# Loading and measuring the image ahead of a frequency-domain layer, and eight even halves on the way back

## The chip, the cores and the metric

One core of a Trainium2 chip runs the whole program in one launch. The metric is the device time of one execution in microseconds: median 3509.49 us of three runs (3507.69 to 3510.06). All times inside an execution are counted from the start of the profiled span.

## The reference

The input x has the shape (4, 128, 128, 16). Four residual blocks follow, each behind a group normalisation (8 groups of two channels, mean and variance over image and pair):

```python
x = x + _L0_conv_ref(_gn(x), h0, numerators, denumerator)   # 2D rational filter, applied by FFT
x = x + _L1_conv_ref(_gn(x), Wq, bq, ...)                    # 8x8 patches, products in frequency
x = x + _L2_conv_ref(_gn(x), filters, bias)                  # 3x3 convolution
x = x + _L3_conv_ref(_gn(x), h0, numerators, denumerator)    # as the first, other weights

def _L0_conv_ref(x, h0, numerators, denumerator):
    a = jnp.pad(denumerator, ..., constant_values=1.0); b = jnp.pad(numerators, ...)
    h = irfft2(rfft2(b, s=(128, 128)) / rfft2(a, s=(128, 128)))
    H_full = h0 + rfft2(h, s=(256, 256))[0]
    Y = einsum('...hwi,ijhw->...hwj', rfft2(x, s=(256, 256)), H_full)
    return irfft2(Y)[..., :128, :128, :]
```

## The kernel before

The program is a row of stages. Each stage has a block of its own with one instruction list per engine (PE, ACT, DVE, POOL, and SP, which issues DMAs); between stages all engines meet at a barrier, and the semaphores of the stage are cleared. Inside a stage the order on an engine is the order of the list, and a wait on a semaphore holds everything behind it on that engine. DMAs issued by SP travel in queue q1, those issued by ACT in q10; both use the same 16 DMA engines.

**build_filters** (0 to 637 us) computes the filters of both layers in 16 units: per unit ACT splits spectra out of PSUM (den, sq), POOL and DVE form the quotient, PE turns it back to lags and to slots, ACT puts the slots into `stage` (L400), and SP stores `stage` to DRAM, eight pieces of 512 KB a unit (L239). The two units of pair p are `stage[:, 0]` and `stage[:, 1]`; the last unit is pair 7, half 1. At its end SP waits for all stores to land (L255).

**filtered_layer** runs as layer 0 and as layer 1. Its start: SP loads the image (layer 0 only; in layer 1 the local convolution leaves it in SBUF) and the constants (L682 to L686); ACT loads the filters of the first two groups, eight DMAs of 256 KB (L938); DVE takes the statistics, 32 bn_stats (L870); PE averages them over partitions (L755, L759) with small DVE operations between, ACT takes the root (L941), DVE the reciprocal (L886). Then 32 rows: PE transposes a channel (L745), DVE normalises it into `cols` (L892), PE transforms it (L766), ACT copies the row out (L946), and SP stores it as two DMAs of 136 KB (L660; some late rows share the work with ACT). Four row buffers are in the ring: row v waits until the DMAs of row v - 4 have landed. From these rows in DRAM the shifted copies are loaded, and 32 groups of convolution products follow on PE (L774, L788), each with filters fetched by SP (L562).

On the way back the last products are moved across partitions by eight small DMAs (L670). PE (L821) forms 16 units, each an even half and an odd half of four products, into PSUM banks; six even halves are done ahead of the moved products, and then six odd halves and ten whole units; DVE adds each unit to the image (L930).

**to_patches** and **patch_mixer** (the second block) lie between the layers, and **local_conv** before layer 1: 16 tiles, each a convolution on PE (L1818, L1822), a sum on DVE (L1858), a transposition (L1809), and a copy to the image on ACT (L1790).

Of the kernel before, what the change touches and what calls it, by code (L numbers as in the profile page):

```python
# [123 lines left out]
GROUPS = L // 4  # L124
# [18 lines left out]
def build_filters(nc, io, scratch, const):  # L143
# [10 lines left out]
    with ExitStack() as ctx:  # L154
# [7 lines left out]
        den = sb("den", [128, DEEP, 8, 2, PAIRS])  # L162
        sq = sb("sq", [128, DEEP, 8, 2, PAIRS])
        mag = sb("mag", [128, DEEP, 8, PAIRS])
        rec = sb("rec", [128, DEEP, 8, PAIRS])
        straight = sb("straight", [128, DEEP, 8, 2, PAIRS])
        crossed = sb("crossed", [128, DEEP, 8, 2, PAIRS])
        nyq = sb("nyq", [128, 2, PAIRS])
        spec = sb("spec", [L, 2, 2, PAIRS, FW])
        lags = sb("lags", [128, 2, 2, L // LAGS, C, LAGS], R32)  # L170
        stage = sb("stage", [128, 2, GROUPS, 4, KB, 4])
# [16 lines left out]
        stored = [sem(f"stored{k}") for k in range(2)]  # L188
# [30 lines left out]
        def _(sp):  # L219
# [13 lines left out]

            def store(pair, jp, piece):

                if piece == 0:
                    sp.wait_ge(far_out, KB * (2 * pair + jp + 1))
                at = slice(GROUPS // PIECES * piece, GROUPS // PIECES * (piece + 1))
                sp.dma_start(scratch["filters"][at, :, pair, jp].rearrange("g p n -> p g n"),  # L239
                             stage[:, jp, at].rearrange("p g m k s -> p g (m k s)")).then_inc(stored[jp], 16)  # L240
# [199 lines left out]
        def _(dve):  # L440
# [67 lines left out]
            for g in range(8):  # L508
                lags_rest(UNITS - 1, g)

# [49 lines left out]

def load_filters(eng, filt, scratch, layer, g, k, q):
# [23 lines left out]
def filtered_layer(nc, layer, image, source, spare, filt, scratch, const, out_dram, tag):  # L585
# [22 lines left out]
    with ExitStack() as ctx:  # L608
        sb, ps, sem = allocators(nc, ctx, tag)
        ident = sb("ident", [128, 128])  # L610
        average = sb("average", [128, 128])
        fwd_w = sb("fwd_w", [L, 2, 128])
        inv_w = sb("inv_w", [128, 2, L])
        eps = sb("eps", [128, 1])
        stats = sb("stats", [128, 32, 6])
# [15 lines left out]
        direct = [ps(f"direct{k}", [128, B, FAR + 2]) for k in range(2)]  # L631
# [3 lines left out]
        img = [a[:].rearrange("p (j g) t -> p j (g t)", j=4) for a in (*acc[0], *acc[1])]  # L635

        image_in = [sem(f"image_in{b}") for b in range(B)]
        consts_in, stats_ready, zeroed = sem("consts_in"), sem("stats_ready"), sem("zeroed")
# [101 lines left out]
        def _(pe):  # L740
# [7 lines left out]
            pe.wait_ge(consts_in, 48)  # L748
            if source is not None:
                for b in range(B):  # L750
                    pe.wait_ge(image_in[b], 16)
            for i in range(4):
                turn_channel(i)
            pe.wait_ge(stats_ready, 1)
# [107 lines left out]
        def _(dve):  # L862
# [3 lines left out]
            for n in range(32):  # L866
                b, g = n // 8, n % 8
                if source is not None and g == 0:
                    dve.wait_ge(image_in[b], 16)
# [63 lines left out]
        def _(act):  # L933
            if source is not None:
                act.wait_ge(image_in[B - 1], 16)
# [985 lines left out]
```

## Time and profile before

| | us |
|---|---|
| median of three runs | 3509.49 |
| the profiled execution | 3497.7 |
| its span | 3495.9 |
| PE busy in the span | 3244.6 (93%) |
| filter stage, up to the first instruction of layer 0 | 0 to 637 |
| layer 0: start and rows / groups / way back | 637 to 706 / to 1122 / to 1160 |
| local convolution, up to the first instruction of layer 1 | to 2980.5 |
| layer 1: start and rows / groups / way back | to 3045 / to 3453 / to 3491 |

A window row gives busy time and instruction count per engine, then the granted TensorE clock (1.00 is 2.4 GHz, 0.50 is 1.2 GHz), the mean busy share of the 16 DMA engines, and GB/s. A timeline row gives the start, the duration from the first start to the last end of merged instructions, engine, line, operation, count, and in brackets the idle time before and what ended it. SPq and ACTq are DMA issues of SP and ACT.

### The profile page before, as it was taken

To read this page: it belongs to the slowest core of one execution; us is meant where nothing else is said; L and a number is where in the kernel's file an instruction comes from. 1 tells how busy PE (TensorE), PEld (TensorE's weight loads), DVE (VectorE), ACT (ScalarE), POOL (GpSimd) and SP (SyncE) were. 2 spreads that over 40 slices of the span, in tenths; PEclk is the share of its full clock that TensorE was granted. 3 is DMA by queue.
4 is the path that set the end of the run, shared out by engine and by line. 5 is a ranking of instruction groups with operands and counts; after the bars stand their busy time and mean duration, and the time that the engine had idled before them with its cause. 6 is when DMAs were issued, how large, how long until landed. Compare 5 with 4: busy or idle time off the path is not lost. (4 is left out here: it accounts for less than half of the span.)

```text
span 3495.9 us, 82613 instructions
## 1 busy us (share of the span) xinstructions
PE 3244.6 (93%) x37272; PEld 2672.4 (76%) x37272; DVE 1568.7 (45%) x1926; ACT 1680.7 (48%) x1763; POOL 1257.6 (36%) x1018
## 2 busy tenths in 40 slices
PE   7999999589998699999899999999989997799998
PEld 6999998379998566666688776666668773489998
DVE  6787877411111434444765444344665444411112
ACT  3666665356553344444554434444454440355551
POOL 6888886055552102222440001222271000165550
PEclk9999999899999899999999999999999998899999
DMA  0333334787777321222133331222222344777776
GB/s 18 114 116 118 122 122 140 215 209 197 198 196 183 106 94 66 79 73 75 70 109 97 109 121 62 83 73 73 73 73 73 91 126 87 176 204 202 203 202 163
DMA packets 259721, 428.86 MB, mean 123 GB/s; under 512 B 28263, under 2 KB 106601, under 8 KB 257897
## 3 DMA queue, kind: packets, MB, share of 16 engines
q1 hardware_dynamic: 244346, 396.86, 38.9%
q10 hardware_dynamic: 15024, 26.72, 2.4%
q8 instruction: 293, 4.80, 0.6%
q14 instruction: 58, 0.48, 0.0%
HBM read 306.07 MB, written 113.77 MB: 120 GB/s over the span
## 5 line engine op out<-in xcount | busy, mean ns | idle before, releaser
L138 PE MATMUL m_bank<-xn,w 128*128 128x512 f32 x1536 | 619.2, 403 | 31.8 <-DVE m_store L1597 11.7
L139 PE MATMUL m_bank<-xn,w 128*128 128x512 f32 x1536 | 603.1, 393 | 0.0
L140 PE MATMUL m_bank<-xn,w 128*128 128x512 f32 x1536 | 602.8, 392 | 0.0
L774 PE MATMUL c_acc<-c_shifted,filt 128*32 128x256 f32 (+8 forms) x11264 | 457.2, 317 | 9.5 <-issue 9.4
L774 PEld LDWEIGHTS c_acc<-c_shifted,filt 128*32 128x32 f32 x11264 | 442.7, 159 | 20.3 <-issue 16.9
L568 POOL TENSOR_TENSOR filt<-filt 64x1408 f32<-64x1408 f32 x64 | 259.6, 4056 | 473.1 <-DMA filt<-filters_dram 473.1
L581 ACT ACTIVATE filt<-filt 64x2048 f32<-64x2048 f32 (+3 forms) x256 | 422.6, 1754 | 14.3 <-DMA filt<-filters_dram 10.6
L138 PEld LDWEIGHTS m_bank<-xn,w 128*128 128x128 f32 x1536 | 291.3, 190 | 172.9 <-issue 76.0
L129 ACT ACTIVATE w<-raw_weights 128x2048 fp32r<-128x2048 f32 x96 | 373.0, 3886 | 103.3 <-PE m_bank L140 102.0
L133 DVE TENSOR_TENSOR w<-raw_weights,w 128x2048 fp32r<-128x2048 f32 x86 | 334.0, 3883 | 159.0 <-ACT w L129 159.0
L140 PEld LDWEIGHTS m_bank<-xn,w 128*128 128x128 f32 x1536 | 291.1, 190 | 62.9
L139 PEld LDWEIGHTS m_bank<-xn,w 128*128 128x128 f32 x1536 | 291.6, 190 | 59.9 <-issue 2.2
L1689 POOL TENSOR_TENSOR m_sums<-m_sums,m_store 128x512 f32<-128x512 f32 x48 | 139.0, 2896 | 519.6 <-DVE m_store L1554 519.6
L908 DVE TENSOR_TENSOR c_both<-c_acc,c_odd 128x256 f32<-128x256 f32 x64 | 36.0, 563 | 469.5 <-ACT c_odd L969 469.5
L482 DVE RECIPROCAL f_rec<-f_mag 128x256 f32<-128x256 f32 x144 | 226.9, 1586 | 22.5 <-POOL f_mag L518 20.7
L129 ACT ACTIVATE m_w_out<-m_qf 128x1024 fp32r<-128x1024 f32 x64 | 131.6, 2056 | 203.3 <-PE m_bank L140 195.9
L1686 POOL TENSOR_TENSOR m_sums<-m_store 128x512 f32<-128x512 f32 x8 | 24.2, 3023 | 526.7 <-DVE m_store L1554 526.7
L297 PE MATMUL f_ring<-f_inv_h,f_spec 128*64 128x128 f32 x1024 | 199.2, 277 | 14.0 <-POOL f_spec L541 14.0
L1547 DVE TENSOR_TENSOR m_pf<-m_bank,m_qf 128x512 f32<-128x512 f32 x128 | 82.5, 686 | 289.1 <-PE m_bank L1267 289.1
L138 PE MATMUL m_bank<-m_u_out,m_w_out 128*128 128x512 f32 x512 | 204.3, 399 | 7.2 <-DVE m_u_out L133 7.2
L133 DVE TENSOR_TENSOR m_w_out<-m_qf,m_w_out 128x1024 fp32r<-128x1024 f32 x64 | 129.0, 2016 | 181.6 <-ACT m_u_out L129 181.6
L969 ACT ACTIVATE c_odd<-c_acc 128x256 f32<-128x256 f32 x64 | 33.1, 517 | 353.6 <-PE c_acc L774 353.6
(182 smaller groups left out, 6763.7 us busy)
## 6 DMA issues: line engine op xcount, KB each, us to landing
c_shifted<-spectrum_dram SPq DMA_DIRECT2D x256, 270.0 KB, 3.9
filters_dram<-f_stage SPq DMA_DIRECT2D x128, 512.0 KB, 3.6
filt<-filters_dram SPq DMA_DIRECT2D x240, 256.0 KB, 4.7
raw_weights<-in_L_conv_Wq SPq DMA_DIRECT2D x16, 2048.0 KB, 8.7
raw_weights<-in_L_conv_Wk SPq DMA_DIRECT2D x16, 2048.0 KB, 8.6
raw_weights<-in_L_conv_Wv SPq DMA_DIRECT2D x16, 2048.0 KB, 8.6
m_qf<-in_L_conv_Wout SPq DMA_DIRECT2D x128, 256.0 KB, 3.9
spectrum_dram<-c_shifted SPq DMA_DIRECT2D x116, 136.0 KB, 2.4
```

Of the source, the lines that this page charges most:

```text
L129: return eng.activation(out, src, ACT.Copy)
L133: return eng.tensor_tensor(out, src, high.bitcast(F32), ALU.subtract)
L138: pe.matmul(out, w[0], x[0], start=first, stop=False)
L139: pe.matmul(out, w[0], x[1], start=False, stop=False)
L140: return pe.matmul(out, w[1], x[0], start=False, stop=last)
L297: nc.tensor.matmul(lo, re, inv_h[:, 0], start=True, stop=False)
L482: nc.vector.reciprocal(rec[:, s, 0:f], mag[:, s, 0:f]).then_inc(rec_ready, 1)
L568: return eng.tensor_tensor(both, even, odd, ALU.add)
L581: return eng.activation(filters_of(filt, k, phases, 1, column, first), filters_of(filt, k, phases, 0, 1 - column, first), ACT.Copy, scale= ...
L774: mm = nc.tensor.matmul(acc[k % 2][phase][32 * s:32 * s + 32, 0:B, LAGS * kb:HALF], filt[:, k, phase, :, :, 4 * kb + s].rearrange("p j c - ...
L1547: op = nc.vector.tensor_tensor(pf[:, k, d], freq[K][d][:], qf[:, k, d], ALU.mult)
L1689: nc.gpsimd.tensor_tensor(sums[:, head], sums[:, head], store[:, head, d], ALU.add).then_inc(added_up, 1)
```

## The change

- Layer 0's image is loaded by SP at the end of the filter stage, once POOL has finished the last quotient; DVE takes the statistics behind its last work there. The constants `ident`, `average`, `fwd_w` come in at the stage's beginning.
- The scratch tensors den, sq, straight, crossed, mag, rec become views of the image, and spec a view of the later `raw_weights`.
- The filter stage no longer waits for its last stores: the last unit's eight pieces are issued by the next stage, four by SP and four by ACT. The first two groups' filters in layer 0 are fetched by ACT behind rows 5 to 12, with a wait for all stores ahead of the first.
- In layer 1 the statistics are taken by DVE within the local convolution, the constants are loaded there, and the first filters are fetched by SP at the layer's start.
- PE averages the statistics first and transposes channels 0 to 3 between the steps; ACT does one root ahead.
- On the way back eight even halves are done ahead (`direct` grows to a whole bank each).

```diff
+def store_filters(eng, scratch, stage, stored, pair, jp, piece):
+    n = GROUPS // 8
+    return eng.dma_start(scratch["filters"][n * piece:n * piece + n, :, pair, jp].rearrange("g p n -> p g n"),
+                         stage[:, jp, n * piece:n * piece + n].rearrange("p g m k s -> p g (m k s)")).then_inc(stored[jp], 16)
...
-        den = sb("den", [128, DEEP, 8, 2, PAIRS])
...
+        held = image[:].rearrange("p b w c -> p (b w c)")
+        den, sq, straight, crossed = (held[:, 2 * size * n:2 * size * (n + 1)].rearrange("p (s f t n) -> p s f t n", s=DEEP, f=8, t=2)
+                                      for n in range(4))
...
             for pair in range(1, UNITS // 2):
                 step(pair, 0)
                 step(pair, 1)
-            for jp in range(2):
-                for piece in range(PIECES):
-                    store(UNITS // 2 - 1, jp, piece)
-            for jp in range(2):
-                sp.wait_ge(stored[jp], 16 * PIECES * UNITS // 2)
+            for piece in range(PIECES):
+                store(UNITS // 2 - 1, 0, piece)
+            sp.wait_ge(spec_ready, UNITS)
+            for b in range(B):
+                sp.dma_start(image[:, b], io["x"][b]).then_inc(image_in[b], 16)
+            sp.wait_ge(tables_in, 48)
...
             for g in range(8):
                 lags_rest(UNITS - 1, g)
+            for b in range(B):
+                dve.wait_ge(image_in[b], 16)
+                image_stats(nc, image, stats, b).then_inc(stats_ready, 1)
+            dve.wait_ge(stats_ready, B)
...
+def image_stats(nc, image, stats, b):
+    for g in range(8):
+        op = nc.vector.bn_stats(stats[:, 8 * b + g], image[:, b, :, 2 * g:2 * g + 2])
+    return op
...
+    LAST_PAIR, FETCH_AT = 7, 5
-    AHEAD = 6
+    AHEAD = 8
...
-        direct = [ps(f"direct{k}", [128, B, FAR + 2]) for k in range(2)]
+        direct = [ps(f"direct{k}", [128, B, L]) for k in range(2)]
...
         @block.sync
         def _(sp):
-            if source is not None:
-                for b in range(B):
-                    sp.dma_start(image[:, b], source[b]).then_inc(image_in[b], 16)
-            sp.dma_start(ident[:], const["ident"]).then_inc(consts_in, 16)
-            sp.dma_start(average[:], const["average"]).then_inc(consts_in, 16)
-            sp.dma_start(fwd_w[:], const["fwd_w"]).then_inc(consts_in, 16)
+            if staged is not None:
+                stage, stored = staged
+                for at in range(4):
+                    store_filters(sp, scratch, stage, stored, LAST_PAIR, 1, at)
+            else:
+                for k in range(EARLY):
+                    for q in range(4):
+                        load_filters(sp, filt, scratch, layer, k, k, q).then_inc(filt_in[k], 16)
             sp.dma_start(inv_w[:], const["inv_w"]).then_inc(inv_in, 16)
...
-            for i in range(4):
-                turn_channel(i)
-            pe.wait_ge(stats_ready, 1)
             nc.tensor.matmul(tot.rearrange("p (n s) -> p n s", s=2), average[:],
                              stats[:].rearrange("p n (s k) -> p n s k", k=3)[:, :, :, 1], start=True, stop=True).then_inc(sum_ready, 1)
+            turn_channel(0)
+            turn_channel(1)
             pe.wait_ge(mean_ready, 1)
             pe.wait_ge(spread_ready, 1)
             nc.tensor.matmul(tot, average[:], spread[:].rearrange("p n s -> p (n s)"), start=True, stop=True).then_inc(sum_ready, 1)
+            turn_channel(2)
+            turn_channel(3)
...
         @block.scalar
         def _(act):
-            if source is not None:
-                act.wait_ge(image_in[B - 1], 16)
-            for k in range(EARLY):
-                for q in range(4):
-                    load_filters(act, filt, scratch, layer, k, k, q).then_inc(filt_in[k], 16)
+            if staged is not None:
+                stage, stored = staged
+                for at in range(4, 8):
+                    store_filters(act, scratch, stage, stored, LAST_PAIR, 1, at)
+            act.wait_ge(zeroed, 1)
+            nc.scalar.activation(warm[:], eps[:], ACT.Sqrt)
             act.wait_ge(var_ready, 1)
...
                 nc.scalar.activation(rows[:, v % 4, :, :, LAGS:], freq[v % 2].rearrange("p b (t q) -> p b q t", q=2), ACT.Copy).then_inc(rows_ready, 1)
+                if staged is not None and FETCH_AT <= v < FETCH_AT + 4 * EARLY:
+                    if v == FETCH_AT:
+                        for jp in range(2):
+                            act.wait_ge(stored[jp], 16 * 8 * (LAST_PAIR + 1))
+                    k, q = divmod(v - FETCH_AT, 4)
+                    load_filters(act, filt, scratch, layer, k, k, q).then_inc(filt_in[k], 16)
...
+            def take_stats(b):
+                dve.wait_ge(moved, 4 * b + 4)
+                image_stats(nc, image, stats_2, b).then_inc(image_ready, 1)
+
             for t in range(16):
...
+                if t % 4 == 2 and t > 4:
+                    take_stats(t // 4 - 1)
+            take_stats(B - 1)
+            dve.wait_ge(image_ready, B)
```

In `build`, stage, the tables and the semaphores `stored` are now opened around `build_filters` and handed to the layer; `img[u % 6]` becomes `img[u % 8]`, with the two banks of `direct` as the seventh and eighth.

## Rows read from the trace of the kernel before

**Rows 1.** Windows: length, busy us of PE, PEld, DVE, ACT, POOL, clock, DMA share, GB/s.

```profile
80.00:600.00 520.00, 502.32 (x6530) 469.95 (x6531) 416.41 (x632) 340.64 (x663) 426.63 (x681) 1.00 0.36 121
...
640.00:680.00 40.00, 26.11 (x100) 16.79 (x100) 32.20 (x100) 10.40 (x17) 6.34 (x2) 0.74 0.87 235
```

**Rows 2.** Timeline, ACT, 610 to 669: start us, us, engine, line, operation, idle before.

```profile
610.98 11.19 ACT L400 ACTIVATE f_stage<-f_ring 128x512 f32<-128x512 f32 x16 [1.79 <-PE f_ring L314]
...
649.34 5.31 ACTq L562 DMA_DIRECT2D filt<-filters_dram  x8
...
654.74 1.28 ACT L941 ACT_TABLE_LOAD   x1 [32.56 <-issue]
...
656.03 0.32 ACT L941 ACTIVATE c_std<-c_var,c_eps 128x32 f32<-128x32 f32 x1
...
668.30 0.60 ACT L946 ACTIVATE c_shifted<-c_acc 128x512 f32<-128x512 f32 x1 [0.71 <-PE c_acc L766]
```

**Rows 3.** Timeline of SP's queue (SPq), 622 to 694, the stores by narrow windows.

```profile
622.20 2.02 SPq L239 DMA_DIRECT2D filters_dram<-f_stage  x3
...
625.60 2.73 SPq L239 DMA_DIRECT2D filters_dram<-f_stage  x2
...
629.73 1.36 SPq L239 DMA_DIRECT2D filters_dram<-f_stage  x1
...
660.93 32.42 SPq L660 DMA_DIRECT2D spectrum_dram<-c_shifted  x46
```

**Rows 4.** Timeline of DVE, same stretch.

```profile
609.23 0.69 DVE L133 TENSOR_TENSOR f_lags<-f_ring,f_lags 128x512 fp32r<-128x512 f32 x1 [1.05 <-ACT f_lags L129]
...
641.83 10.55 DVE L870 BATCH_NORM_STATS2 c_stats<-image 128x6 f32<-128x256 f32 x32 [4.53 <-DMA image<-in_x]
...
656.78 6.47 DVE L892 TENSOR_SCALAR raw_weights<-c_acc,c_mean,c_rstd 128x128 f32<-128x128 f32 x20
```

**Rows 5.** Windows of 2 us, 602 to 671, for the DMA columns.

```profile
602.00:604.00 2.00, 2.00 (x40) 2.00 (x38) 0.70 (x2) 0.81 (x2) 0.00 (x0) 1.00 0.37 124
...
624.00:626.00 2.00, 0.00 (x0) 0.00 (x0) 0.00 (x0) 0.00 (x0) 0.00 (x0) 1.00 1.03 339
...
641.00:643.00 2.00, 0.00 (x0) 0.00 (x0) 1.17 (x4) 0.00 (x0) 0.00 (x0) 0.50 1.00 418
...
655.00:657.00 2.00, 0.41 (x2) 0.30 (x2) 0.95 (x4) 1.34 (x2) 0.00 (x0) 1.00 1.07 199
...
669.00:671.00 2.00, 2.00 (x9) 1.18 (x8) 2.00 (x7) 0.69 (x2) 0.00 (x0) 1.00 0.96 216
```

**Rows 6.** Timeline of DVE, ACT, SP: local convolution's end, start of layer 1.

```profile
2942.40 1.11 DVE L1858 SCALAR_TENSOR_TENSOR l_res<-l_acc,l_bias,l_xt 128x512 f32<-128x512 f32 x1 [2.77 <-PE l_acc L1822]
...
2979.14 0.60 ACT L1790 ACTIVATE image<-l_turn 128x512 f32<-128x512 f32 x1 [0.81 <-PE l_turn L1809]
...
2980.55 0.34 SPq L683 DMA_DIRECT2D c_ident<-const_ident  x1
...
2981.12 10.20 DVE L870 BATCH_NORM_STATS2 c_stats<-image 128x6 f32<-128x256 f32 x31
...
2995.87 6.47 DVE L892 TENSOR_SCALAR spare<-c_acc,c_mean,c_rstd 128x128 f32<-128x128 f32 x20
```

**Rows 7.** Timeline of PE and DVE on the way back, and two clock windows.

```profile
1133.46 25.87 PE L821 MATMUL c_acc<-c_inv_w,filt 128*128 128x128 f32 x208 [4.11 <-DMA filt<-raw_weights]
...
3463.66 26.39 PE L821 MATMUL c_acc<-c_inv_w,filt 128*128 128x128 f32 x208 [4.83 <-DMA filt<-spare]
...
3475.80 0.69 DVE L930 TENSOR_TENSOR image<-image,c_acc 128x512 f32<-128x512 f32 x1 [1.10 <-PE c_acc L821]
...
1131.00:1132.00 1.00, 0.00 (x0) 0.00 (x0) 0.00 (x0) 0.00 (x0) 0.00 (x0) 0.84 0.08 6
...
3462.00:3463.00 1.00, 0.00 (x0) 0.00 (x0) 0.00 (x0) 0.00 (x0) 0.00 (x0) 0.99 0.00 0
```

**Rows 8.** Timeline of POOL in the filter stage.

```profile
589.17 0.72 POOL L526 TENSOR_TENSOR f_crossed<-f_crossed 128x256 f32<-128x256 f32 x1
```

More of the change, by code:

```diff
@@ L161, in build_filters @@
         respread = sb("respread", [L, 2, 2 * 128], R32)
-        den = sb("den", [128, DEEP, 8, 2, PAIRS])
[L163 to L167, printed above, removed]
+        ident_0, average, fwd_w, stats = tables
+        held = image[:].rearrange("p b w c -> p (b w c)")
+        size = DEEP * 8 * PAIRS
+        den, sq, straight, crossed = (held[:, 2 * size * n:2 * size * (n + 1)].rearrange("p (s f t n) -> p s f t n", s=DEEP, f=8, t=2)
+                                      for n in range(4))
+        mag, rec = (held[:, size * n:size * (n + 1)].rearrange("p (s f n) -> p s f n", s=DEEP, f=8) for n in range(8, 10))
         nyq = sb("nyq", [128, 2, PAIRS])
-        spec = sb("spec", [L, 2, 2, PAIRS, FW])
+        spec = spare[:].rearrange("p a r n -> p (a r n)").rearrange("p (k c n f) -> p k c n f", k=2, c=2, n=PAIRS)
         lags = sb("lags", [128, 2, 2, L // LAGS, C, LAGS], R32)
-        stage = sb("stage", [128, 2, GROUPS, 4, KB, 4])
         early = stage[:].rearrange("p j g m k s -> p (j g m k s)")
@@ L187, in build_filters @@
         far_ready, far_out = sem("far_ready"), sem("far_out")
-        stored = [sem(f"stored{k}") for k in range(2)]
+        tables_in, stats_ready = sem("tables_in"), sem("stats_ready")
+        image_in = [sem(f"image_in{b}") for b in range(B)]
         block = ctx.enter_context(nc.Block())
@@ L582, in lower_columns, with filtered_layer @@
                           scale=1.0 if column else -1.0)
-def filtered_layer(nc, layer, image, source, spare, filt, scratch, const, out_dram, tag):
+def filtered_layer(nc, layer, image, tables, staged, spare, filt, scratch, const, out_dram, tag):
     N_BATCHES = GROUPS // RING
@@ L865, in _ @@
             nc.vector.memset(odd[:, :, :, 0:1], 0.0).then_inc(edge_set, 1)
[L866 to L869, printed above, removed]
-                op = nc.vector.bn_stats(stats[:, n], image[:, b, :, 2 * g:2 * g + 2])
-            op.then_inc(stats_ready, 1)
             sample = stats[:].rearrange("p n (s k) -> p n s k", k=3)
@@ L1716, in _, with local_conv @@
                     normalise(half, n)
-def local_conv(nc, io, image, scratch, const, tag):
+def local_conv(nc, io, image, tables, scratch, const, tag):
     with ExitStack() as ctx:
@@ L1871, in build @@
     }
-    build_filters(nc, io, scratch, const)
     with nc.sbuf_tensor("mean1", [128, B], F32) as mean, nc.sbuf_tensor("rstd1", [128, B], F32) as rstd:
         with nc.sbuf_tensor("raw_weights", [128, 2, 8, 512], F32) as raw:
-            with nc.sbuf_tensor("image0", [128, B, L, C], F32) as image:
+            with ExitStack() as ctx:
+                sb, ps, sem = allocators(nc, ctx, "a_")
+                image = sb("image0", [128, B, L, C])
+                tables = tables_tensors(sb)
+                stored = [sem(f"stored{k}") for k in range(2)]
+                with nc.sbuf_tensor("stage", [128, 2, GROUPS, 4, L // 8, 4], F32) as stage:
+                    build_filters(nc, io, image, raw, tables, stage, stored, scratch, const)
                 with filter_tensor(nc, "filt0") as filt:
-                    filtered_layer(nc, 0, image, io["x"], raw, filt, scratch, const, None, "c0_")
+                    filtered_layer(nc, 0, image, tables, (stage, stored), raw, filt, scratch, const, None, "c0_")
             with nc.sbuf_tensor("xn", [128, 2, 8, N], R32) as x:
@@ L1881, in build @@
                     patch_mixer(nc, io, x, (w0, w1), mean, rstd, raw, scratch, const, "m_")
-    with nc.sbuf_tensor("image1", [128, B, L, C], F32) as image:
-        local_conv(nc, io, image, scratch, const, "l_")
+    with ExitStack() as ctx:
+        sb, ps, sem = allocators(nc, ctx, "e_")
+        image = sb("image1", [128, B, L, C])
+        tables = tables_tensors(sb)
+        local_conv(nc, io, image, tables, scratch, const, "l_")
         with filter_tensor(nc, "filt1") as filt:
             with nc.sbuf_tensor("spare", [128, 2, 8, 512], F32) as spare:
-                filtered_layer(nc, 1, image, None, spare, filt, scratch, const, out, "c3_")
+                filtered_layer(nc, 1, image, tables, None, spare, filt, scratch, const, out, "c3_")
 INPUTS = {
```

37 lines of the change are left out of this document (18 added, 19 removed).

## The prediction

> **What bounds the kernel now.** I read the busy time by stage first, then the chain of waits, then each engine's timeline around the places that the diff touches. The groups of convolution products and the second block are PE work that the change leaves alone. The stretches with slack are the seams. In the filter stage PE is busy for 502 of 520 us; in the 40 us at layer 0's start only 26 of 40, at a mean clock of 0.74 [rows 1].
>
> Read as a chain, that seam is one thing after the other: ACT puts the last slots out until 622.17 (610.98 + 11.19) [rows 2]; SP then issues eight stores of 512 KB, the last ending at 631.09 [rows 3], and waits until they land; only then is the image loaded; DVE, waiting for it, takes statistics from 641.83 to 652.38 and begins to normalise at 656.78 [rows 4]. From there to the first products the row phase is paced by row stores: SP issues 46 without a pause, 0.70 us each [rows 3]. So the bound at this seam is DMA, then DVE, then DMA.
>
> At layer 1 the same statistics stand alone between the local convolution's last copy (ends at 2979.74) and the normalisation at 2995.87 [rows 6]. On the way back PE waits 4.11 and 4.83 us for the moved products, and then runs 208 matmuls in 25.87 and 26.39 us [rows 7].
>
> **Part 1, layer 0's start: -25.9 us.** The image is loaded behind the eight stores of the last unit but one. Their transfer ends in the window 602 to 604 (124 GB/s there against 339 at full rate, so at 602.7); the image, 4.19 MB at 418 GB/s, takes 10.0 us [rows 5], to 612.7. DVE is free at 609.92 and needs 32 x 0.33 = 10.55 us [rows 4], so it ends at 620.5, under ACT's slots, which end at 622.17. The cover is thin, 1.7 us on DVE and about 5 on the image's last quarter (wanted at 617.8); past that, each microsecond late costs one.
>
> The next stage then starts at 622.17 plus a barrier. From ACT's end at 2979.74 to the first DMA of layer 1 is 0.81 us [rows 6], so 622.98. The stores of the last unit are no longer waited for, but four of them now stand in ACT's list ahead of the root. This is the term without a row. From below: on one queue the fifth store begins to issue 3.4 us after the first (622.20 to 625.60). From above: all eight take 8.9 us (to 631.09) [rows 3]; two queues that drain together at one queue's rate could hold ACT that long. I take 5.6, nearer to the lower end, since four and not eight stand in the ring. Behind them come the table load 1.28, the extra root 0.32, and from the true root to the first normalisation 0.75 (656.03 to 656.78) [rows 2, 4]: 622.98 + 5.6 + 2.35 = 630.93 against 656.78, a gain of 25.85 (22.5 to 28.0). PE and DVE's own chain isn't later: from the end of the statistics to 656.78 were 4.40 us, so about 627.4, or 629.2 with two more channels transposed in between. The new root ahead of the true one saves nothing here, since ACT is late anyway.
>
> **Part 2, the first filters move into the row phase: +8.3 us.** Before, eight fetches of 256 KB were issued at 649.34 [rows 2] while PE and DVE were in the statistics. Now they come behind rows 5 to 12. The wait ahead of them is free: row 5 comes 11.5 us behind the first normalisation (668.30 against 656.78 [rows 2, 4]), so about 642, and 4.19 MB of stores at 339 GB/s [rows 5] are done near 636. ACT's issue costs 5.31 / 8 = 0.66 us in an idle of 0.71 per row [rows 2]: nothing, but for some tenths. The filters themselves are wanted only by row 19.
>
> What isn't free is the transfer. Alone, the fetch ran at 199 GB/s with the DMA engines' share at 1.07; the row stores ran at 216 GB/s and 0.96 [rows 5]. From above it costs its whole length, 2.10 MB / 199 GB/s = 10.5 us. From below nothing: a share of 0.96 for one queue need not mean that two queues can't overlap. I take the additive case with the little room there is, 0.11 of each microsecond over some 20 us: 10.5 - 2.2 = 8.3. The row stores queue behind it on SP, ACT's row copies wait for stores four rows back, and PE for ACT; nothing later in the phase is idle enough to win it back.
>
> The Trainium skill bears on this (DMA: Bandwidth & Descriptors, section "Issuing engines are not separate DMA queues"): DMAs of different issuers end on the same 16 engines and interleave, and a second issuer saves issue time alone. The two shares of rows 5 fit it, but no row shows these two transfers at once. By the rule part 2 costs its 8 to 10 us; without it, nothing.
>
> **Part 3, layer 1's start: -8.2 us.** Three of the four images' statistics run in DVE's idle time under the convolution: 8 x 0.33 = 2.64 us against 2.77 us idle per tile [rows 4, 6]. If they run over, PE wants the next sum only one tile of 3.88 us (1.11 + 2.77) later, so still nothing. The last image's eight wait for ACT's last copy: 2979.74 + 2.7 = 2982.45, plus the barrier 0.81, plus the chain of 4.40 us as in layer 0 [rows 4]: 2987.66 against 2995.87. The four constants' loads and ACT's fetch no longer stand in front; the fetch, now on SP's queue, is issued in 8 x 0.66 us, before the first row is ready. Bounds 7.0 (PE still cold from its pause) to 9.5 (PE no longer behind four channels).
>
> **Part 4, the way back, twice: -7.8 us.** Two more even halves, 16 matmuls, move into the wait. Warm, a whole unit of 16 takes 0.69 + 1.10 = 1.79 us [rows 7]; that much goes per layer. The wait itself ends with the moved products, as before. PE's idle time shrinks to 2.32 and 3.04 us. The clock counts here: 208 matmuls at the warm pace are 23.2 us, so 2.6 and 3.2 of the 25.87 and 26.39 are paid at the 1.2 GHz level. It fell 2.35 us behind PE's last matmul in layer 0 (1133.46 - 4.11 = 1129.35; 0.84 granted from 1131 to 1132, so at 1131.7) and 4.15 us in layer 1 (0.99 in the last microsecond to 3463) [rows 7]. In layer 0 I let it stay up (1.79 + 2.6 = 4.4), in layer 1 count the half (1.79 + 1.6 = 3.4). Bounds: 3.6 if it falls in both, 9.4 if in none. DVE's adds of 0.69 still fit under halves of 0.89. The wider `direct` banks cost nothing that a row shows.
>
> **The sum.** 25.85 - 8.3 + 8.2 + 7.8 = 33.6 us off the profiled execution's 3497.7 (span 3495.9): 3464.1. The runs' median, 3509.49, stands 11.8 above the profiled one; taking the same off it gives **3475.9 us**, which I forecast.
>
> **Rivals.**
> - *The fetch hides.* Two queues overlap and part 2 costs nothing: gain 41.9, **3467.6**. For it: the share is summed over queues, and 1.07 shows that their packets can overlap. Against: at 1.07 the rate was lower, 199 GB/s.
> - *ACT is held to the end.* Its four stores are out only after 8.9 us, the fetch costs all of 10.5, the clock falls in both waits: 22.5 - 10.5 + 7.0 + 3.6 = 22.6, **3486.9**. For it: issues of 1.36 us each at the end of the burst [rows 3].
> - *The statistics don't fit.* The image lands late, the stage is held and part 1 shrinks. With half of it gone the gain is 20.7, **3488.8**; with all, 7.7, **3501.8**. Against: 5 us of room.
> - *Slower: the moved scratch tensors slow the filter stage.* den to rec now lie in the image, spec in the later weights' buffer. POOL is busy for 426.6 of 520 us there [rows 1]; if its operations were dearer at the new places, 512 us of stage would stretch. The gain of 33.6 is gone from 6.6% on; at 10%, 51 us are lost: **3527**. Against it: POOL's operations take the same 0.72 us [rows 8] on tensors at quite different places.
>
> **Chances.** Forecast (3471 to 3482) 0.47; fetch hidden (3462 to 3471) 0.28; ACT held (3482 to 3488) 0.14; statistics late (3488 to 3502) 0.05; slower 0.04; about nothing in all, 0.02. No change means within 0.2%, 7.0 us, about what a measurement of this kernel can tell. So faster 0.94, same 0.02, slower 0.04. The range of 8 in 10 is 3463 to 3487: the first three cases but for their outer edges.
>
> **What would show it.** Part 1: DVE's bn_stats end before ACT's last slot copy, and the first normalisation comes 8 us (5.7 to 11.5) behind the stage's start. Part 2: row stores at a pitch well over 0.70 us, or a longer landing, in the rows behind row 5; if the pitch holds, the first rival is right. Part 3: the first normalisation of layer 1 about 8 us behind ACT's last image copy. Part 4: 192 matmuls behind the wait, in 21.5 us if the clock reads 1.00 throughout. The forecast is wrong if the filter stage's end moves off 622, or if the distance from the first normalisation to the first product of layer 0 shrinks or grows by more than part 2 says.

## The result, and the profile after

The kernel after took 3461.34 us (median of four runs, 3458.84 to 3469.81) against 3508.59 (four runs, 3500.11 to 3510.06): a ratio of 0.9868, with an interval of 0.9841 to 0.9895. Two later timings gave 0.9868 (0.9831 to 0.9905) and 0.9889 (0.9847 to 0.9930). All 14 runs of the kernel after in these three have a median of 3468.1, all 25 of the kernel before (in these and beside the kernels of the experiments) one of 3508.5: some 40 us faster, where I forecast 33.6. The first timing, which I had forecast at 3475.9, lies just under my range of 3463 to 3487.

Single profiles scatter by 10 us and more, so the steps are read from distances inside a profile. First the seam at layer 0, in windows of the kernel after (columns as in [rows 1]):

```profile
80.00:600.00 520.00, 502.32 (x6530) 469.93 (x6531) 416.37 (x632) 340.80 (x663) 426.24 (x681) 1.00 0.36 121
612.00:652.00 40.00, 32.56 (x177) 23.27 (x176) 29.25 (x94) 18.31 (x32) 2.73 (x1) 0.96 0.74 233
```

The filter stage is as it was, POOL's 426 us too, so the rival in which the moved scratch tensors slow it is dead. The seam has PE busy for 32.6 of 40 us at a clock of 0.96, where [rows 1] had 26.1 at 0.74. The timeline of ACT, SP's queue and DVE there, against [rows 2 to 4]:

```profile
610.91 11.06 ACT L410 ACTIVATE stage<-f_ring 128x512 f32<-128x512 f32 x16 [1.78 <-PE f_ring L324]
622.86 3.64 ACTq L146 DMA_DIRECT2D filters_dram<-stage  x4
626.53 1.28 ACT L954 ACT_TABLE_LOAD   x1 [4.55 <-issue]
...
627.93 0.30 ACT L956 ACTIVATE c_std<-c_var,c_eps 128x32 f32<-128x32 f32 x1
...
598.64 4.31 SPq L264 DMA_DIRECT2D a_image<-in_x  x4
...
632.81 35.70 SPq L682 DMA_DIRECT2D spectrum_dram<-c_shifted  x46
...
609.77 10.54 DVE L577 BATCH_NORM_STATS2 a_stats<-a_image 128x6 f32<-128x256 f32 x32
...
624.98 0.23 DVE L899 TENSOR_REDUCE c_var<-c_direct 128x32 f32<-128x64 f32 x1 [0.59 <-PE c_direct L778]
...
628.66 9.01 DVE L907 TENSOR_SCALAR raw_weights<-c_acc,c_mean,c_rstd 128x128 f32<-128x128 f32 x28
```

The statistics end at 620.3, under ACT's copies of the last slots. The variance is there at 625.2, but ACT comes to the root only at 627.93, behind its four stores. The normalisation starts at 628.66 (656.78 before). SP's 46 row stores take 35.70 us where [rows 3] had 32.42. PE's first product of the layer, before and then after, ends the row phase:

```profile
706.12 8.10 PE L774 MATMUL c_acc<-c_shifted,filt 128*32 128x256 f32 x176
```

```profile
680.27 7.29 PE L795 MATMUL c_acc<-c_shifted,filt 128*32 128x256 f32 x174
```

It comes 49.34 us behind the first normalisation before (656.78 to 706.12) and 51.61 after (628.66 to 680.27). Layer 1's start, against [rows 6]:

```profile
2957.05 0.60 ACT L1815 ACTIVATE e_image<-l_turn 128x512 f32<-128x512 f32 x1 [0.80 <-PE l_turn L1834]
...
2964.50 0.32 ACT L956 ACTIVATE c_std<-c_var,c_eps 128x32 f32<-128x32 f32 x1 [2.49 <-DVE c_var L899]
...
2955.22 1.09 DVE L1888 SCALAR_TENSOR_TENSOR l_res<-l_acc,l_bias,l_xt 128x512 f32<-128x512 f32 x1 [0.15 <-PE l_acc L1847]
2957.68 2.71 DVE L577 BATCH_NORM_STATS2 e_stats<-e_image 128x6 f32<-128x256 f32 x8 [1.38 <-ACT e_image L1815]
...
2965.25 2.96 DVE L907 TENSOR_SCALAR spare<-c_acc,c_mean,c_rstd 128x128 f32<-128x128 f32 x9
```

From ACT's last image copy to the normalisation are 7.60 us where [rows 6] had 16.13. Statistics of three images fit under the convolution: on the tiles behind them DVE's idle time ahead of the sum falls from 2.77 to 0.15, and the tiles keep their pace of 3.88. The way back in layer 0: first ACT's copy of the last group's odd products out of PSUM (called the last odd copy below) and DVE's last add to the image, before and then after.

```profile
1117.37 0.45 ACT L969 ACTIVATE c_odd<-c_acc 128x256 f32<-128x256 f32 x1 [13.02 <-PE c_acc L774]
...
1159.36 0.69 DVE L930 TENSOR_TENSOR image<-image,c_acc 128x512 f32<-128x512 f32 x1 [1.10 <-PE c_acc L821]
```

```profile
1097.38 0.45 ACT L990 ACTIVATE c_odd<-c_acc 128x256 f32<-128x256 f32 x1 [13.04 <-PE c_acc L795]
...
1137.15 0.69 DVE L945 TENSOR_TENSOR a_image<-a_image,c_direct 128x512 f32<-128x512 f32 x1 [1.10 <-PE c_direct L842]
```

From the start of the one to the end of the other are 42.68 us before and 40.46 after. PE's timeline there in the kernel after, and two clock windows, against [rows 7]:

```profile
1113.81 7.22 PE L842 MATMUL c_acc<-c_inv_w,filt 128*128 128x128 f32 x48 [3.92 <-DMA filt<-raw_weights]
...
1112.00:1113.00 1.00, 0.00 (x0) 0.00 (x0) 0.00 (x0) 0.00 (x0) 0.00 (x0) 1.00 0.00 0
...
1115.00:1116.00 1.00, 1.00 (x7) 1.00 (x6) 0.69 (x1) 0.00 (x0) 0.00 (x0) 0.50 0.00 0
```

PE still stands idle for 3.92 us (3.84 in layer 1), and the clock still falls to 0.50 behind it. Last, the DMA queues in 22 us of the row phase, before and then after: packets, MB and the share of the 16 engines' time that these packets took, and the issues with KB each and median us to landing (in the kernel after q10 holds the fetch).

```profile
q1 hardware_dynamic: 2463, 4.31, 87.1%
...
spectrum_dram<-c_shifted SPq DMA_DIRECT2D x32, 136.0 KB, 2.4
```

```profile
q1 hardware_dynamic: 2323, 4.05, 63.4%
q10 hardware_dynamic: 1152, 2.10, 32.8%
...
spectrum_dram<-c_shifted SPq DMA_DIRECT2D x30, 136.0 KB, 4.3
filt<-filters_dram ACTq DMA_DIRECT2D x8, 256.0 KB, 4.9
```

Nearly half as many bytes again went through in the same 22 us. Beside the fetch the row stores' packets take less of the engines' time, 3.4 us per MB (0.634 x 22 / 4.05) where alone they took 4.4, though each store lands later, 4.3 us behind its issue where it was 2.4.

### The profile page after: what moved, and what is told of

It is laid out like the page before. It is cut to its first block and busy times, and to the rows that moved or that the text cites. A ratio compares the mean times of both kernels' runs of the same rounds, so it can differ in the third digit from the quotient of the medians.

```text
span 3468.0 us, 82637 instructions
## 1 busy us (share of the span) xinstructions
PE 3237.8 (93%) x37272; PEld 2664.2 (77%) x37272; DVE 1565.3 (45%) x1926; ACT 1677.5 (48%) x1765; POOL 1250.9 (36%) x1018
## 5 line engine op out<-in xcount | busy, mean ns | idle before, releaser
L795 PE MATMUL c_acc<-c_shifted,filt 128*32 128x192 f32 (+8 forms) x11264 | 457.6, 317 | 21.5 <-issue 21.5
L492 DVE RECIPROCAL a_image<-a_image 128x256 f32<-128x256 f32 x144 | 226.9, 1585 | 22.4 <-POOL a_image L532 20.8
L307 PE MATMUL f_ring<-f_inv_h,raw_weights 128*64 128x128 f32 x1024 | 199.1, 276 | 14.0 <-POOL raw_weights L555 14.0
```

Source lines behind the costliest of these rows:

```text
L307: nc.tensor.matmul(lo, re, inv_h[:, 0], start=True, stop=False)
L492: nc.vector.reciprocal(rec[:, s, 0:f], mag[:, s, 0:f]).then_inc(rec_ready, 1)
L795: mm = nc.tensor.matmul(acc[k % 2][phase][32 * s:32 * s + 32, 0:B, LAGS * kb:HALF], filt[:, k, phase, :, :, 4 * kb + s].rearrange("p j c - ...
```

## The experiments

Edits are to the kernel after unless said otherwise; each profile is a single execution. "Row phase" is the distance from a layer's first normalisation to its first product: 49.34 us in layer 0 before and 51.61 after, 48.88 and 48.63 in layer 1.

**fetch_first.** Is the fetch the reason for the 2.3 us?

```diff
 for at in range(4, 8):
     store_filters(act, scratch, stage, stored, LAST_PAIR, 1, at)
+for jp in range(2):
+    act.wait_ge(stored[jp], 16 * 8 * (LAST_PAIR + 1))
+for k in range(EARLY):
+    for q in range(4):
+        load_filters(act, filt, scratch, layer, k, k, q).then_inc(filt_in[k], 16)
...
-    load_filters(act, filt, scratch, layer, k, k, q).then_inc(filt_in[k], 16)   # behind row v
```

> Undoes part 2 alone: in layer 0 ACT waits for the last unit's stores and issues the eight filter fetches ahead of the root, as before the change, and none in the row phase. All three theories of the fetch agree that the first normalisation comes late (stores landed near 638.5, eight issues of 0.66, table load, roots: about 646.5 against 628.66) and that the distance from the first normalisation to the first product falls back to the 49.3 us that it had before. They differ in what that says: 49.3 against 51.6 would make 2.3 us the whole price of the fetch in the row phase, where I had forecast 8.3. If the distance stays near 51.6, the 2.3 us have nothing to do with the fetch.

Measured: normalisation at 648.72, row phase 49.20. ACT's list, then SP's row stores:

```profile
626.77 3.64 ACTq L146 DMA_DIRECT2D filters_dram<-stage  x4
641.25 5.30 ACTq L586 DMA_DIRECT2D filt<-filters_dram  x8
...
652.87 32.55 SPq L682 DMA_DIRECT2D spectrum_dram<-c_shifted  x46
```

SP is back at 32.55 us for 46 stores. So the fetch in the row phase has a price, and it is this small. What ACT waits for in the row phase says where it is paid, in the kernel after (us in total, times, longest) and then with the fetch ahead:

```profile
ACT c_shifted L961 <- DMA spectrum_dram<-c_shifted: 12.2, 10, 2.9
ACT c_shifted L961 <- PE c_acc L787: 10.2, 10, 4.0
```

```profile
ACT c_shifted L966 <- PE c_acc L787: 16.3, 18, 4.0
ACT c_shifted L966 <- DMA spectrum_dram<-c_shifted: 3.5, 4, 2.2
```

Row stores that land later hold ACT's copies 8.7 us longer, and 6.1 us of that are time in which ACT would have waited for PE anyway: cover that my forecast did not count.

**store_more.** Twice the extra traffic, the second half in the direction of the row stores; nothing reads what it stores.

```diff
+    if staged is not None and FETCH_AT + 8 <= v < FETCH_AT + 16:
+        act.dma_start(scratch["dump"][:, m], image[0:64, m // 2]...)   # 256 KB
```

> Adds 2.10 MB of stores (eight of 256 KB, image to a scratch tensor in DRAM, so SBUF to DRAM like the row stores) behind rows 13 to 20 of layer 0, issued by ACT as the fetch is behind rows 5 to 12. Additive theory (the DMA engines are full at a share of 0.96): 2.10 MB at 216 GB/s, 9.7 us, so 61.3 us from the first normalisation to the first product against 51.6. Direction theory (a fetch overlaps with stores because it goes the other way, stores among themselves don't): the same 9 to 10 us, 60 to 61.5. Ceiling theory (the engines carry some 350 GB/s whatever the direction, and the row stores alone ask for only 216): again about the 2.3 us that the fetch cost, 53.5 to 55.

Measured: 56.48, 4.9 more than after; 341 GB/s at a share of 1.04 over 12 us. That is half of what the additive and the direction theories want, and 1.5 us over the ceiling theory's upper end.

**fetch_four.** The filters of four groups ahead in place of two.

```diff
-EARLY = 2
+EARLY = 4
...
-for m in range(8):
-    if m:
-        sp.wait_ge(progress, m)
-    piece(sp, 2, 2, m)
-    if m >= 4:
-        piece(sp, 3, 3, m - 4)
+for m in range(4, 8):
+    sp.wait_ge(progress, m)
+    piece(sp, 2, 2, m)
```

> Fetches the filters of the first four groups ahead instead of two: 16 fetches behind rows 5 to 20 in layer 0, 16 on SP ahead of the rows in layer 1; the loads of groups 2 and 3 behind the row phase keep only the rows. Additive theory: another 10.5 us in layer 0's row phase, 62 us from the first normalisation to the first product. Ceiling theory: another 2 to 3 us, 53.5 to 55. Layer 1: 0 to 3 us on its 48.6. The next groups, 18.1 and 20.6 us apart in layer 0 and 16.5 and 17.3 in layer 1 against some 12.4 later, come 3 to 8 us sooner in all if the filters' loads held them up, not sooner if the rows' loads did.

Measured: 55.43 in layer 0, 3.8 more than after, so sixteen fetches cost 6.2 us and not 21. The next two groups of layer 0 come 11.2 and 13.8 us apart, 13.7 sooner in sum. Layer 1's row phase took 60.39, 11.8 more, which I had not expected. ACT's timeline there:

```profile
2970.90 1.27 ACT L958 ACTIVATE c_shifted<-c_acc 128x512 f32<-128x512 f32 x2 [14.02 <-DMA spectrum_dram<-c_shifted]
```

Sixteen fetches ahead on the stores' own queue (4.19 MB at some 207 GB/s, 20 us) held the first row stores back until they were through: the first one, issued at 2957.22, landed 12.0 us later, when the last fetches landed too.

**fetch_sp.** The same eight fetches, issued by SP between its row stores.

```diff
-    load_filters(act, filt, scratch, layer, k, k, q).then_inc(filt_in[k], 16)
...
     store_rows(sp, v, par, i, c)
+if staged is not None and FETCH_AT <= v < FETCH_AT + 4 * EARLY:
+    load_filters(sp, filt, scratch, layer, k, k, q).then_inc(filt_in[k], 16)
```

> The same eight fetches behind the same rows 5 to 12 of layer 0, but issued by SP, in the queue that carries the row stores, where the change has ACT issue them. The run with four groups gave the reason to ask: in layer 1 sixteen fetches on SP's queue ahead of the rows held ACT for 14 us on a row store, at 207 GB/s in all, while from ACT's queue the same sixteen cost 3.8 us more than eight. Queue theory (one queue's transfers go one after the other, a second queue's go beside them): the fetch costs its length here, 2.10 MB at 199 GB/s or 10.5 us less what little SP has spare, so 57 to 61 us from the first normalisation to the first product against 51.6 (two runs: 51.6 and 52.4). Ceiling theory (only the sum of bytes counts, up to some 350 GB/s): 52 to 54, plus at most 8 issues of 0.66 us, so a pure cost of issuing would show as 54.5.

Measured: 55.32, 3.7 more than after. SP's queue in that stretch:

```profile
645.24 0.63 SPq L586 DMA_DIRECT2D filt<-filters_dram  x1
645.92 1.24 SPq L682 DMA_DIRECT2D spectrum_dram<-c_shifted  x2
647.20 0.62 SPq L586 DMA_DIRECT2D filt<-filters_dram  x1
```

A fetch takes 0.68 us of SP's list (645.24 to 645.92); eight times that is 5.4 of the 6.0 us over 49.34. The result lies 1.7 us under the queue theory's range and 0.8 over the 54.5 that I gave for a pure cost of issuing. So interleaved with the stores the fetch overlaps on one queue too, and most of its price there is issue time.

**split_rows.** Layer 1 alone.

```diff
-return v > LAST_EVEN and v % 2 == 1
+return (v > LAST_EVEN or staged is None) and v % 2 == 1
```

> Layer 1 alone: the second store of every odd row is issued by ACT from the first row on (before, from row 21 on), so SP issues 3 stores for two rows where it issued 4. If SP's issue of 0.70 us each paces the row phase, two rows fall from 2.8 towards 2.1 us, and layer 1's distance from the first normalisation to the first product falls from 48.6 by up to 7 us, to 41.5 to 45, with a higher rate of bytes. If the DMA engines do (share 0.96 at 216 GB/s), it stays at 48.6, and the issues on SP get no shorter in sum. The first says that there was room for the fetch all along.

Measured: 46.24, 2.4 less than after. SP's stores of the first 24 rows, 36 now and 46 before, took 30.48 us where they took 32.21, and ACT's wait for row stores fell from 8.3 us to 1.7 while that for PE rose from 10.5 to 14.8. So PE's own pace is close below that of the stores: a second issuer wins some 2 us, not 7. (Nine profiles with layer 1's start as in after have 47.8 to 50.5 us there, so 46.24 is below them all, but only by 1.5.)

**stores_sp.** The term that I had bounded without a row: ACT held by its stores.

```diff
-for at in range(4): store_filters(sp, ...)
+for at in range(8): store_filters(sp, ...)
...
-for at in range(4, 8): store_filters(act, ...)
```

> All eight stores of the last unit on SP, none on ACT. In the kernel after, the variance was ready at 625.2 and ACT, held by its four stores and the table load, took the root at 627.93. With ACT free the root follows the variance: the first normalisation comes 3.1 us behind the next stage's start, where it was 5.8, so 2.7 us sooner. If the chain on DVE and PE is the limit all along, it does not move. SP's issues end near 9 us behind the stage's start, about when the first row is ready, so at most 1 us of it is lost to the first row stores.

Measured: the normalisation comes 3.39 us behind the stage's start where it was 5.81, as expected. But the row phase took 56.47, 4.9 more. SP's queue and ACT:

```profile
623.83 8.92 SPq L146 DMA_DIRECT2D filters_dram<-stage  x8
632.79 1.36 SPq L710 DMA_DIRECT2D c_inv_w<-const_inv_w  x1
...
640.05 1.30 ACT L959 ACTIVATE c_shifted<-c_acc 128x512 f32<-128x512 f32 x2 [3.99 <-DMA spectrum_dram<-c_shifted]
```

My "at most 1 us" was wrong. SP is not free for the first row store before 634.15, and that store is issued 6.98 us behind the first normalisation where it was 4.15; the first rows then land behind eight big stores on their queue. The normalisation gained 2.4 us and the row phase lost 4.9, so ACT's being held is the cheaper of the two.

**ahead_six.** Six even halves ahead, as before the change.

```diff
-AHEAD = 8
+AHEAD = 6          # and img[u % 6]
```

> Undoes part 4 alone: six even halves ahead in place of eight, in both layers. My forecast had 4.4 and 3.4 us for it; the two profiles showed 2.2 and 2.0 from the last odd copy to the last add. So 42 to 43 us there in each layer against 40.5 and 40.8, 208 matmuls behind the wait in 25 to 26.5 us, PE's idle time 4.5 to 5.5 (1.8 more, plus what the moved products' landing varies by). If the two banks more are worth nothing, 40.5 to 41 stays.

Measured from the last odd copy to the last add: 43.05 and 42.41. Both profiles of before have 42.68 and 42.87, 43.48 and 43.22; three of after 40.46 and 40.83, 39.90 and 44.17, 40.62 and 39.17. So the two banks are worth about 2.7 us in layer 0 and 1.4 in layer 1 (means of three). The split between the layers is within the scatter: all ten profiles with eight ahead and no filler, those of the other experiments included, average 41.3 and 40.6, which makes it 1.8 and 2.3. The sum is about 4 us either way.

**fill_wait.** Matmuls without a result in PE's wait, as filler.

```diff
 for u in range(3, AHEAD):
+    if u == AHEAD - 1:
+        for _ in range(4):
+            for j in range(4):
+                nc.tensor.matmul(img[u][:, j], prod[:, 0, j, 0:L], inv_w[:, 0], start=j == 0, stop=j == 3)
     back(u, 0)
```

> Four more even halves of matmuls in PE's wait on the way back, into a bank that the last even half then clears (they add no result). PE's idle time ahead of the second halves, 3.92 and 3.84 us, falls to 0 to 0.5. If the clock fell because PE was idle, it now stays at 1.00 and the 192 matmuls take 21.5 us where they took 23.3, so each way back is some 1.8 us shorter. If the clock falls all the same, 23.3 stays. If the wait was shortened by something else than the moved products' landing, it would now be longer by what the filler overruns.

PE's timeline and a clock window in layer 0 (L857 is the filler):

```profile
1109.63 3.74 PE L857 MATMUL c_direct<-c_inv_w,filt 128*128 128x128 f32 x32
...
1114.09 5.52 PE L842 MATMUL c_acc<-c_inv_w,filt 128*128 128x128 f32 x48
...
1114.00:1115.00 1.00, 1.00 (x12) 1.00 (x11) 0.00 (x0) 0.00 (x0) 0.00 (x0) 1.00 0.00 0
```

The clock stays at 2.4 GHz, and 48 matmuls take 5.52 us where they took 7.22: 1.7 us, as expected. But PE no longer waits for the moved products, so the filler overran: the way back took 40.47 and 40.21, as without it. The profiled execution lost 22 us in the mixer (below).

**after_2, before_2, four_and_fill.** The first two are the two kernels once more. The last is the kernel after with EARLY = 4, the fetch of groups 2 and 3 of layer 1 on ACT behind rows 5 to 12, and three even halves of filler on the way back.

```diff
+first_here = 0 if staged is not None else 2
-if staged is not None and FETCH_AT <= v < FETCH_AT + 4 * EARLY:
+if FETCH_AT <= v < FETCH_AT + 4 * (EARLY - first_here):
...
+    k += first_here
```

> The kernel after, once more, for a second profile and a narrower interval. The forecast's steps, as the first profiles showed them (25 to 28 us at layer 0's start, 8 to 11 from the mixer's start to layer 1's normalisation, 3 to 4 on the two ways back, less 2 to 3 for the fetch), sum to 36 to 40 us; the first timing says 46 (38 to 56). Theory one: the steps are all, and the interval comes down to 36 to 42 us (ratio 0.988 to 0.990). Theory two: some 8 us more are gained where the change was not meant to act, in the convolution groups, and it stays at 44 to 48 (0.9865 to 0.9875).

> The kernel before, once more, for a second profile. The first one's span was 11 us under the runs' median. If its convolution groups were the luck (402.3 us from the first odd copy to the last in layer 0, 395.2 in layer 1; profiles of the changed kernel have 393 to 409), this one shows 3 to 12 us more there, and the same 49 us from normalisation to first product, 42.7 and 42.9 on the way back, and 34 us from ACT's last slot copy to the first normalisation.

> The kernel after with the two edits that paid in their own segments: filters of four groups ahead (in layer 0 from ACT behind rows 5 to 20; in layer 1 two groups on SP ahead of the rows, as after, and two from ACT behind rows 5 to 12), and three even halves of filler in the wait on the way back. From the first normalisation to the third odd copy, layer 0 had 98.6 us in the kernel after and 89.0 with four groups; layer 1 had 93.0, and with the extra fetch beside the rows and not ahead of them should have 48.6 + 3 + 8.5 + 25.9 = 86 to 88. The filler gives 0.5 to 1.7 us a layer. In sum 13 to 19 us below the kernel after, about 3446. If the first groups were held by bytes and not by the order of the loads, layer 1's gain is lost and the sum is 8 to 11.

Measured: after_2 0.9868 (median 3469.70), within theory two by its number, though the interval holds both. before_2 took 3508.48, 10.8 us above the first profile: 3.6 from the end of the filter stage (625.74 where it was 622.18), 2.9 and 2.4 in the groups, the rest in small parts; from ACT's last slot copy to the normalisation it has 34.65 us and in the row phase 49.48, as expected. So what the first profile had by luck was spread, not in the groups alone. four_and_fill: 0.9850 (0.9807 to 0.9892), median 3463.01: 6.7 us below after_2, where I had expected 13 to 19. Its profiled execution (3477.35) lost 22 us in the mixer, at the same place as fill_wait's; its other three runs took 3461.22 to 3463.78, so whether each execution loses them is not known. DVE there, POOL, and POOL in after_2:

```profile
1722.12 25.28 DVE L133 TENSOR_TENSOR w<-raw_weights,w 128x2048 fp32r<-128x2048 f32 x1 [3.17 <-ACT w L129]
...
1704.44 39.39 POOL L1724 TENSOR_TENSOR m_store<-m_store,m_pf 128x512 f32<-128x512 f32 x29 [3.64 <-DVE m_pf L1609]
```

```profile
1708.65 57.03 POOL L1721 TENSOR_TENSOR m_store<-m_store,m_pf 128x512 f32<-128x512 f32 x29 [3.64 <-DVE m_pf L1606]
```

**four_beside, after_3.** The former is four_and_fill without the filler.

> The run with four groups and filler without the filler: four groups' filters ahead, in layer 0 from ACT behind rows 5 to 20, in layer 1 two groups from SP ahead of the rows and two from ACT behind rows 5 to 12; AHEAD at eight as in the kernel after. Both profiles with filler had one VectorE operation in the mixer at 25.3 us that takes 3.8 to 4.9 us in every other profile, and lost some 22 us between layer 0's last add and layer 1's normalisation. Theory one (a matter of how the filler shifts the mixer, or of the filler itself): here that distance is 1824 to 1828 us again, and the whole is 11 to 15 us below the kernel after in the same call. Theory two (fetching four groups ahead does it, or it comes by chance): the 22 us show here too. Layer 0 from first normalisation to third odd copy 89 us (98 in the kernel after), layer 1 84 to 86 (93 to 95).

> The kernel after a third time, on the chip of the run beside it. The profiles' steps sum to 37 to 39 us. If that is all, the ratio to before is 0.988 to 0.990 and before's profiles and times on this chip agree with it; if the first two timings hold (0.9868 each), some 5 to 8 us of the gain lie outside the steps. Distances: 50.7 to 52.4 us from layer 0's first normalisation to its first product, 1824 to 1828 from layer 0's last add to layer 1's normalisation.

Measured: four_beside 3448.55 (0.9822, 0.9777 to 0.9867), after_3 3470.72 (0.9889) on the same chip: the four groups beat both kernels, by 22 us against after, where I had expected 11 to 15. The two intervals overlap, but five of the six runs of four_beside are faster than every run of after_3. From the first normalisation to the third odd copy layer 0 took 88.2 us and layer 1 85.5, against 95.7 and 94.3 in after_3, 16 of the 22 us. The mixer's distance is 1823.8, as theory one has it: the loss of 22 us shows in both profiles with filler and in none of the other thirteen. after_3 lies within theory one's range of its own, 0.988 to 0.990, but its interval holds 0.9868 as well; the two timings alone don't decide.

## Why the prediction was right and wrong

| step | forecast | measured, before | after |
|---|---|---|---|
| 1: ACT's last slot copy to normalisation | -25.9 | 34.60, 34.65 | 6.69, 6.70, 6.71 (-27.9) |
| 2: row phase of layer 0 | +8.3 | 49.34, 49.48 | 51.61, 50.71, 50.68 (+1.6) |
| 3: last image copy to normalisation, layer 1 | -8.2 | 16.13 | 7.60 (-8.5) |
| 4: last odd copy to last add, both layers | -7.8 | 85.55, 86.70 | 81.29, 84.07, 79.79 (-4.4) |

In sum -39 us against -33.6 forecast and some -40 by the pooled runs, so the steps account for the gain. The first timing lies 14.6 us under the forecast. The steps explain 5.6 of that: 6.7 from part 2, 2.0 from part 1 and 0.3 from part 3, less 3.4 from part 4. The other 9 stand in no step and go with the scatter: the three timings differ in their medians by 47.3, 40.0 and 35.7 us.

**The step that failed is part 2**: "I take the additive case with the little room there is, 0.11 of each microsecond over some 20 us: 10.5 - 2.2 = 8.3". It cost 1.6 us by these profiles, and 2.0 in the mean of all six that share this code (50.68 to 52.42). Two things in it were wrong. I took the share of one window of 2 us, 0.96 [rows 5], for the phase; over 32 us of the row stores it was 0.85:

```profile
661.00:693.00 32.00, 29.17 (x94) 14.04 (x94) 19.28 (x58) 16.70 (x25) 3.17 (x1) 0.95 0.85 195
```

That is the smaller fault: with 0.85 the same sum would still have given 6.1 (10.5 - 0.22 x 20). The larger is that the shares did not add. A busy packet is partly a waiting packet here: the fetch's took 5.0 us per MB alone (0.855 x 12 / 2.06) and 3.4 beside the stores (0.328 x 22 / 2.10). The 12 us around the fetch in the kernel before, by queue, and a window of the kernel after with both:

```profile
q10 hardware_dynamic: 1122, 2.06, 85.5%
```

```profile
642.00:654.00 12.00, 10.18 (x40) 5.46 (x38) 8.35 (x26) 3.93 (x7) 3.18 (x1) 1.00 1.02 316
```

At 4.4 and 5.0 us per MB the two would have filled 1.29 of the engines' time (4.05 x 4.4 + 2.10 x 5.0 = 28.3 of 22 us); measured were 0.96. fetch_first shows the price, store_more and fetch_four that twice the bytes cost 6 to 7 us and not 20, fetch_sp that it isn't the second queue that does it.

So the DMA engines, which I had called the bound of the row phase, were not full. What paced the row stores seems to be SP's issuing. Seven of them by narrow windows, in the kernel before, and in the kernel after as the fetch starts:

```profile
675.75 4.45 SPq L660 DMA_DIRECT2D spectrum_dram<-c_shifted  x7
```

```profile
639.57 4.58 SPq L682 DMA_DIRECT2D spectrum_dram<-c_shifted  x7
```

The median distance from one issue to the next is 0.64 us in both kernels, though a store landed 4.3 us behind its issue beside the fetch and 2.4 without, so landing does not set it. My reading of [rows 3], 46 stores "without a pause, 0.70 us each", took a merged row for an unbroken one: it holds pauses of SP of 2.9 us in sum, and the 35.70 us after hold 5.3. My first rival had this mechanism; its condition, a pitch held at 0.70 us, is met by the single issue and not by the mean (35.70 / 46 = 0.78). That a second issuer takes 2.4 us off (split_rows), and that the same fetches cost more on SP's list than on ACT's (fetch_sp), fits.

The Trainium skill's rule that I cited (DMA: Bandwidth & Descriptors, section "Issuing engines are not separate DMA queues") stands: transfers of the two issuers interleave, and a second issuer saves issue time alone. The runs agree: issuing from ACT and not from SP saved 3.7 us (51.61 against 55.32) of the 5.4 that the eight issues take on SP. The rule does not say that the two transfers add in length; it was my reading of the share that made 8 us of it. Another page of the Trainium skill (Perfetto Trace Analysis, section "Identifying the Most-Contended Engine") says to judge DMA by how much of the memory's bandwidth is used and not by occupancy, since 16 engines make occupancy misleading; the trace agrees, 195 GB/s at 0.85 and 316 at 1.02.

**Part 1** was right in its order of events, and 2 us too small: ACT's four stores took 3.64 us, near my lower end of 3.4, not 5.6. **Part 3** was right to 0.3 us. **Part 4** was too large by 3.4. I let PE's idle time shrink by a whole unit, 1.79 us, and the clock stay up in layer 0. In the first profile of after the idle time is 3.92 and 3.84 us, where it was 4.11 and 4.83. In layer 0 PE had paused for 1.01 us among its even halves before the change, as its timeline shows; this profile of after has no such pause, so its even halves end only half a microsecond later behind the issue of the moved products (6.5 where it was 6.0), and not 1.79:

```profile
1126.52 2.83 PE L821 MATMUL c_acc<-c_inv_w,filt 128*128 128x128 f32 x23 [1.01 <-issue]
```

And the moved products let PE go on 10.4 and 10.3 us behind their issue (10.1 and 9.5 before). So the clock fell in both layers of this profile, the case that I had priced at 3.6; the two distances shrank by 4.3. The later profiles show that chance plays into it. The pause is back in after_2, 2.07 us in layer 0 and 4.86 in layer 1, and the latter used up the gain (44.17). In two of the six ways back of the three profiles, after_2's layer 0 and after_3's layer 1, the clock stayed at 1.00, and the 192 matmuls took 21.7 us where they took 23.3 in the first profile. What makes the pause is left open. That the clock stays up when PE has work in place of the idle time is what fill_wait shows.

That the errors of parts 1 and 4 nearly cancel is luck: with 1.6 for the fetch the sum would have been 40.3, what the 25 and 14 runs show.

## What to carry to other kernels

Take a DMA share from the whole stretch in which the new transfer will run, and ask how many bytes per second the engines have carried elsewhere in the trace (418 GB/s for the image in [rows 5]); here a share near 1 at half that rate was in good part waiting, not work. A row of the timeline that merges many issues can hide pauses: look at single issues before calling a queue busy throughout. The big transfers of this kernel cost by where they stood: spread out one per row, sixteen of them cost 6.2 us of the 21 that their length would have been; in a burst ahead of small ones on the same queue they held these back by 4 and 14 us. Read steps of a few microseconds from distances between fixed instructions, since whole runs of this kernel scatter by 10 us and more.

## What the runs showed of the hardware that I had not expected

In both profiles with filler one DVE operation of the mixer, an operation on two tensors in SBUF that takes 3.8 to 4.9 us elsewhere, took 25.3. It ended 3.6 us behind the end of POOL's run of adds in both (1704.44 + 39.39 = 1743.83, and 1747.40, in four_and_fill), so it seems to have stood still until POOL was done; POOL's 29 adds took 39.4 us, where they took 57.0 when the two alternated. The Trainium skill (SBUF — State Buffer, section "Who interferes with whom") says that a DVE instruction with two inputs in SBUF contends with a GpSimd (POOL) instruction that reads SBUF, over a shared port pair that it calls an exclusive lock. The trace agrees, and here the wait seems to have lasted for a whole row of POOL's instructions, 21.7 us (1722.12 to 1743.83). How the filler, 600 us earlier, brings the two into this step is not shown.
